# Attention values in a decoder layer: the high part of the probabilities times high and low values as one product of 128 columns

## What is computed

```python
x = x + attention(layernorm(x))
x = x + experts(layernorm(x))

# attention, for each sequence
q = ((h @ Wqa) @ Wqb)            # 16 heads of 64 + 64 (the second 64 rotated by position)
c_kv, k_pe = split(h @ Wkva)     # 64 latent values, 64 rotated keys per token
k, v = split(c_kv @ Wkvb)        # per head
scores = q @ k.T * scale         # causal
probs = softmax(scores)
out = (probs @ v) @ Wo
```

## Time and profile before

| | us |
|---|---|
| median of 3 runs | 1811.85 |
| lowest, highest | 1811.03, 1813.68 |
| profiled execution | 1815.64 |
| its span | 1813.8 |

### The profile page before, as it was taken

One profiled execution on the slowest core, in us unless ns is written; L12 is line 12 of the kernel. 1 busy time (PEld: TensorE's weight loads), 2 busy tenths in 40 slices (PEclk: granted clock), 3 DMA queues, 4 the chain that ended last, 5 costly groups with the idle time before them and its releaser, 6 DMA issues.

```text
span 1813.8 us, 45737 instructions
## 1 busy us (share of the span) xinstructions
PE 1549.9 (85%) x16420; PEld 1100.6 (61%) x16421; DVE 1311.4 (72%) x2969; ACT 1031.2 (57%) x2344; POOL 984.9 (54%) x1597
## 2 busy tenths in 40 slices
PE   7755788999878999998799999987999999889980
PEld 3233566766756667666567676665676666556650
DVE  1365886788768878887678788876877888555546
ACT  1343555666556666666566666664666666556650
POOL 3023566756457777554767756447776444343430
PEclk9777899999999999999999999998999999999995
DMA  6247441322234433123454321234432311356318
GB/s 167 76 110 109 80 72 38 56 57 57 53 74 83 94 63 60 23 51 59 76 102 74 63 55 39 36 64 92 86 60 57 57 30 25 99 148 210 114 32 280
DMA packets 333670, 144.19 MB, mean 79 GB/s; under 512 B 277168, under 2 KB 328403, under 8 KB 333398
## 3 DMA queue, kind: packets, MB, share of 16 engines
q1 hardware_dynamic: 308624, 105.54, 29.4%
q10 hardware_dynamic: 17926, 19.02, 3.6%
q0 software_dynamic: 6912, 16.83, 2.9%
HBM read 46.78 MB, written 29.53 MB: 42 GB/s over the span
## 4 chain that ended last, share of the span: by engine, by line
PE 51%; DVE 22%; ACT 6%; issue 6%; SPq 3%; DMA 3%; POOL 3%; DVEq 1%; ACTq 0%; POOLq 0%
PE of_ps L643 20%; PE s_ps L643 18%; PE t_ps L799 10%; DVE pT L1557 6%; DVE smax L1528 3%; ACT pT L989 2%; SPq L437 2%; DVE smax L1532 2%; DVE nmax L1536 1%; PE t_ps L882 1%; DVE nmax L1539 1%; ACT probs L1113 1%; DVE work L1363 1%; PE of_ps L899 1%; DVE smax L1510 1%
## 5 line engine op out<-in xcount | busy, mean ns | idle before, releaser
L1557 DVE TENSOR_TENSOR pT<-t_ps,pT 128x512 f16<-128x512 f32 (+3 forms) x688 | 409.7, 598 | 179.2 <-ACT pT L989 176.2
L989 ACT CAST pT<-t_ps 128x512 f16<-128x512 f32 (+3 forms) x688 | 355.1, 516 | 284.7 <-PE t_ps L799 283.4
L643 PE MATMUL s_ps<-kT,qT 128*128 128x512 f16 (+3 forms) x2304 | 492.5, 328 | 8.1 <-DMA kT<-ks_sb 4.1
L799 PE MATMUL t_ps<-id,probs 128*128 128x128 f32 x2304 | 384.5, 282 | 67.7 <-DVE pT L1557 28.2
L799 PEld LDWEIGHTS t_ps<-id,probs 128*128 128x128 f32 x2304 | 259.1, 143 | 167.5 <-issue 78.5
L1113 ACT ACTIVATE probs<-s_ps,nmax,fac 128x640 f32<-128x640 f32 (+3 forms) x256 | 269.2, 1052 | 2.2 <-DVE nmax L1536 2.2
L643 PE MATMUL of_ps<-weights,xT 128*128 128x512 f16 (+1 forms) x960 | 217.9, 366 | 59.8 <-DVE ks_sb L1352 23.0
L643 PEld LDWEIGHTS of_ps<-ckv,pT 128*128 128x128 f16 x6912 | 241.9, 98 | 42.8 <-DVE o_sb L1391 10.3
L643 PE MATMUL of_ps<-ckv,pT 128*128 128x64 f16 x6912 | 258.8, 193 | 7.9 <-DVE o_sb L1391 7.6
L643 PEld LDWEIGHTS s_ps<-kT,qT 128*128 128x128 f16 x2304 | 218.2, 99 | 76.8 <-issue 5.7
L643 PEld LDWEIGHTS of_ps<-weights,xT 128*128 128x128 f16 x960 | 83.3, 102 | 147.7 <-DVE ks_sb L1352 26.2
(11 more groups left out here) (218 smaller groups left out, 2504.6 us busy)
## 6 DMA issues: line engine op xcount, KB each, us to landing
wgu_sb<-wgu ACTq DMA_DIRECT2D x2, 2816.0 KB, 10.4
work<-lists SPq DMA_DIRECT2D x40, 128.5 KB, 2.1
qT<-lists SPq DMA_DIRECT2D x40, 128.5 KB, 2.1
x_sb<-x SPq DMA_DIRECT2D x32, 128.0 KB, 2.5
x<-x SPq DMA_DIRECT2D x32, 128.0 KB, 2.6
dense<-den SPq DMA_DIRECT2D x32, 128.0 KB, 2.7
weights<-dense ACTq DMA_DIRECT2D x1, 4096.0 KB, 21.5
qT<-y_exp SPq DMA_DIRECT2D x16, 256.0 KB, 5.1
```

Of the source, the lines that this page charges most:

```text
L643: return pe_.matmul(o, a, b, start=start, stop=stop)
L799: last = pe_.transpose(t_ps[:, h, c * P:(c + 1) * P], probs[:, u % 2, g * L + j * P:g * L + (j + 1) * P], id32[:, :])
L989: return act.copy(o, i)
L1557: dve.tensor_tensor(pT[:, u % 2, 1, h, 0:w], t_ps[:, h, 0:w], pT[:, u % 2, 0, h, 0:w], ALU.subtract).then_inc(s.lo_p, 1)
```

## The change

For i = 0 nothing changes in what is computed. For the others, the high part of the probabilities is multiplied with the high and low latent values side by side, one product of 128 columns in place of two of 64; the low part times the high values is added to the first 64 columns, as before. A head now takes 128 columns of `o_ps`, so the bank holds four heads, a quarter of a tile. The output therefore leaves in quarters (`out_quarter`): a reciprocal of 4 sums, a reduction that adds the two columns that lie 64 apart (512 values of PSUM to 256 in `o_sb`), and a multiply of the 256 values in `o_sb`. TensorE waits for a new semaphore, `o_taken`, which the reduction signals; `o_ready` is signalled by the multiply of the second and of the fourth quarter. The first and the third quarter wait for `lo_o`. They get places of their own, "quarter0" and "quarter2"; the second stands where the first half's `out_norm` was, the fourth where the second half's was.

```diff
+def parts(i):
+    return 2 if i == 0 else 4
+def part_of(t, k):
+    return sum(parts(j % TB) for j in range(t)) + k
 LONG = {... "half": (8, 3), "half_hi": (9, 0), "down": (10, 2),
+        "quarter0": (4, 3), "quarter2": (12, 3)}
 MIDDLE = {... "half": (4, 3), "half_hi": (5, 0), "out": (5, 2), "down": (7, 2),
+          "quarter0": (2, 3), "quarter2": (6, 3)}
 SECOND = {... "half": (3, 0), "half_hi": (3, 1), ... "down": (4, 0),
+          "quarter0": (2, 0), "quarter2": (4, 0)}
@@ values
-                if u % (U // 2) == 0 and 2 * t + u // (U // 2) > 0:
-                    pe_.wait_ge(s.o_ready, 2 * t + u // (U // 2))
+                step = U // parts(i)
+                if u % step == 0 and t + u > 0:
+                    pe_.wait_ge(s.o_taken, part_of(t, u // step))
...
-                        for a, b in ((0, 0), (0, 1), (1, 0)):
-                            last = mm(o_ps[:, head * C:(head + 1) * C], pT[:, u % 2, a, h, c * P:(c + 1) * P], ckv[:, b, j, :],
-                                      j == 0 and a + b == 0, j == i and a == 1)
+                        hi, lo = (pT[:, u % 2, a, h, c * P:(c + 1) * P] for a in range(2))
+                        if i == 0:
...
+                        else:
+                            head = o_ps[:, ((u * G + g) % (H // 4)) * 2 * C:][:, 0:2 * C]
+                            mm(head.rearrange("p (b c) -> p b c", b=2), hi, ckv[:, :, j, :], j == 0, False)
+                            last = mm(head[:, 0:C], lo, ckv[:, 0, j, :], False, j == i)
@@ before the experts
-            pe_.wait_ge(s.o_ready, 2 * NT)
+            pe_.wait_ge(s.o_taken, part_of(NT, 0))
@@ vector: behind the multiply of out_norm
+                dve.wait_ge(s.o_ready, half + 1)
+                dve.sem_inc(s.o_taken, 1)
+            def out_quarter(p, k):
+                U, half, at_ = units(p), 2 * p + k // 2, part_of(p, k)
+                dve.wait_ge(s.pv_made, unit_of(p, (k + 1) * (U // 4) - 1) + 1)
+                dve.reciprocal(rsum[:, 0:H // 4], ssum[:, p % 2, k * (H // 4):(k + 1) * (H // 4)]).then_inc(s.o_evs, 1)
+                if k % 2 == 0:
+                    dve.wait_ge(s.lo_o, half)
+                o4 = o_ps.rearrange("p (h b c) -> p h c b", b=2, c=C)
+                to = o_sb[:, (k % 2) * (H // 4) * C:][:, 0:(H // 4) * C].rearrange("p (h c) -> p h c", c=C)
+                dve.tensor_reduce(to, o4, AX_X, ALU.add).then_inc(s.o_taken, 1)
+                dve.wait_ge(s.o_taken, at_ + 1)
+                dve.wait_ge(s.o_evs, at_ + 1)
+                last = dve.tensor_tensor(to, to, rsum[:, 0:H // 4].unsqueeze(2).broadcast_to([P, H // 4, C]), ALU.mult)
+                if k % 2:
+                    last.then_inc(s.o_ready, 1)
+            def out_second(p, hh):
+                if p % TB == 0:
+                    out_norm(p, hh)
+                else:
+                    out_quarter(p, 2 * hh + 1)
@@ vector, side
                 if has(p) and (k, sub) == (0, 3):
-                    out_norm(p, 1)
+                    out_second(p, 1)
+                if t % TB and due("quarter0", t, t, k, sub):
+                    out_quarter(t, 0)
...
                 if due("half", t, t, k, sub):
-                    out_norm(t, 0)
+                    out_second(t, 0)
+                if t % TB and due("quarter2", t, t, k, sub):
+                    out_quarter(t, 2)
```

More of the change, by code:

```diff
@@ L86 @@
 LONG = {"lat": (0, 2), "pe0": (0, 3), "pe1": (1, 2), "q0": (2, 2), "q1": (3, 2), "gate": (5, 2), "up": (6, 2), "out": (7, 2),
-        "half": (8, 3), "half_hi": (9, 0), "down": (10, 2)}
+        "half": (8, 3), "half_hi": (9, 0), "down": (10, 2),
+        "quarter0": (4, 3), "quarter2": (12, 3)}
 MIDDLE = {"lat": (0, 1), "pe0": (0, 2), "pe1": (0, 3), "q0": (1, 2), "q1": (2, 2), "gate": (3, 2), "up": (4, 2), "half": (4, 3),
-          "half_hi": (5, 0), "out": (5, 2), "down": (7, 2)}
+          "half_hi": (5, 0), "out": (5, 2), "down": (7, 2),
+          "quarter0": (2, 3), "quarter2": (6, 3)}
 SECOND = {"lat": (0, 3), "pe0": (1, 1), "half_lo": (1, 1), "pe1": (1, 3), "out": (2, 0), "gate": (2, 1), "q0": (2, 2), "up": (2, 3), "q1": (3, 1),
-          "rope_sum": (3, 0), "half": (3, 0), "half_hi": (3, 1), "rope_hi": (3, 2), "rope_lo": (3, 3), "down": (4, 0)}
+          "rope_sum": (3, 0), "half": (3, 0), "half_hi": (3, 1), "rope_hi": (3, 2), "rope_lo": (3, 3), "down": (4, 0),
+          "quarter0": (2, 0), "quarter2": (4, 0)}
 FIRST_TILE = {"gate": (0, 0), "up": (0, 1), "pe0": (0, 2), "pe1": (0, 3), "lat": (1, 0), "q0": (1, 1), "q1": (1, 2), "out": (1, 3),
@@ L250, in build @@
                    s_made maxs max_ready exp_done p_made hi_p lo_p pv_made sum_done
-                   o_evs o_ready hi_o lo_o oT_in ln2_done x2T_in gate_done hi_h lo_h hT_in
+                   o_evs o_taken o_ready hi_o lo_o oT_in ln2_done x2T_in gate_done hi_h lo_h hT_in
                    lg_done top_s ix_ready pick_s mask_ready slot_s slot_done dense_done
@@ L814, in values @@
                     for c, (g, j) in enumerate(half_tiles(i, h)):
-                        head = (u * G + g) % (H // 2)
-                        for a, b in ((0, 0), (0, 1), (1, 0)):
-                            last = mm(o_ps[:, head * C:(head + 1) * C], pT[:, u % 2, a, h, c * P:(c + 1) * P], ckv[:, b, j, :],
-                                      j == 0 and a + b == 0, j == i and a == 1)
+                        hi, lo = (pT[:, u % 2, a, h, c * P:(c + 1) * P] for a in range(2))
+                        if i == 0:
+                            head = o_ps[:, ((u * G + g) % (H // 2)) * C:][:, 0:C]
+                            mm(head, hi, ckv[:, 0, j, :], True, False)
+                            mm(head, hi, ckv[:, 1, j, :], False, False)
+                            last = mm(head, lo, ckv[:, 0, j, :], False, True)
+                        else:
+                            head = o_ps[:, ((u * G + g) % (H // 4)) * 2 * C:][:, 0:2 * C]
+                            mm(head.rearrange("p (b c) -> p b c", b=2), hi, ckv[:, :, j, :], j == 0, False)
+                            last = mm(head[:, 0:C], lo, ckv[:, 0, j, :], False, j == i)
                 last.then_inc(s.pv_made, 1)
@@ L1386, in out_norm @@
                 dve.reciprocal(rsum[:, :], ssum[:, p % 2, hh * (H // 2):(hh + 1) * (H // 2)]).then_inc(s.o_evs, 1)
-                dve.wait_ge(s.o_evs, half + 1)
+                dve.wait_ge(s.o_evs, part_of(p, hh) + 1)
                 if half > 0:
@@ L1694, in hT_copy @@
                 dve.tensor_copy(m_hT_sb[:, :, :, :].rearrange("p a k n -> p (a k n)"), ot[0:KE, 0:4 * P]).then_inc(s.m_hTs, 1)
-            out_norm(NT - 1, 1)
+            out_second(NT - 1, 1)
             gate_hidden(NT - 2)
```

## The result

| | before | after |
|---|---|---|
| median us | 1812.8 (4 runs, 1811.0 to 1816.8) | 1860.3 (4 runs, 1858.4 to 1864.5) |
| profiled execution, its span | 1815.6, 1813.8 | 1858.7, 1856.9 |

The kernel after is slower: ratio 1.026, with an interval of 1.024 to 1.028. That is +48 us by the medians (47.6) and +43 by the profiled executions. The forecast was +37, its range 1812 to 1900.

The account below looks back on a forecast made before the run. TensorE was taken to bound the kernel, with VectorE close behind in longer tiles. New places 23, old places 16, GpSimd's low part 3, less 5 saved on TensorE, gave +37 us: 1849 from the median, range 1812 to 1900.

Parts of the forecast that it names:

- The saving on TensorE: One value product in place of two, 2240 pairs at 2.6 ns each: 5.8 us saved, taken as 5.
- The strided reduction: Rival: the quarters' reduction reads PSUM values 64 apart at half speed, a quarter takes 2.15 us: 1893; chance 0.16.
- New and old places at rest: Stalls with the multiply unstretched by GpSimd: 16 us at first and third quarters (new), 11 at second and fourth (old).
- The prediction's lower sum: Whole kernel with the multiply at rest and no wait for GpSimd: 16 + 11 - 5.8 = +21 us.
- the walk: At 56 new places, each low part's lateness minus its distance to the following transposes: 23 us, 16 at rest.
- GpSimd's low part: First and third quarters wait for it: 2.7 us in tile 4, first batch, 1 more at its third; 3 taken.
- The stretched multiply: Quarter's multiply of 256 values in SBUF, lengthened beside GpSimd: 0.61 us taken, 0.2 above rest; range 0.41 to 1.0.
- Who waits: Signs: idle time of TensorE's transposes behind L1557 grows some 20 us, ScalarE's wait for the output 13 to 16.
- By tile: Sign: the fifth to seventh tiles of a batch each grow by 1.5 to 2 us, the eighth least.

Follow-up runs that it names:

- the run with the multiply out of GpSimd's way: Kernel after with each quarter's multiply replaced by a one-input reduction of the same 256 values, output left undivided: 1837.0 us, ratio 1.013.
- the run with the late output: Kernel before with VectorE's signal to ScalarE for each half's output given 0.41 us later, TensorE released as before: 1826.8 us, ratio 1.006.
- the inserted steps alone: Kernel before with unused VectorE reductions put in at the 56 new places: 1819.9 us with one each (1.004), 1828.6 with two (1.008).
- both together: Kernel before with two unused reductions at each of 56 new places and the later signal to ScalarE at the old ones: 1868.2 us, ratio 1.020.
- the later session: Kernel after run again word for word, beside one with three narrow products: 1866.7 us, ratio 1.020 to the kernel before.

## Why the prediction was right, and where its sizes were off

**The saving on TensorE** (5 taken): the pace was right, 12 products in 0.67 us. The units' medians give 2 to 3 us that arrive; the runs' own medians differ too much among themselves to confirm it. The remark that TensorE isn't busy all the time was worth half of the term or more, not a sixth.

**The strided reduction**: 658 ns against 680 forecast, so that rival is out. The Trainium skill's rule on PSUM ("Advanced Engine Details and Errata", section Memory Cachelines) would have made it dearer; the trace differs for this read of 512 values by VectorE.

**New and old places at rest**: 16 and 11 forecast, 15 and 8 to 13 measured, each by a run of its own. With 2 to 3 saved by TensorE this gives +20 to 26, and the run with the multiply out of GpSimd's way gave +23. The prediction's lower sum, +21, was this case, so the walk held in its sum. Place by place it did less well (tile 3 at (2, 3) above), and part of the agreement is errors that cancel.

**GpSimd's low part** (3): one wait in the trace, 2.7 us, at tile 4 of the first batch, as forecast; the further 1 us for its third quarter isn't there.

**The stretched multiply** is the mis-sized term. The prediction added 0.2 us to each of the 112 multiplies, 22 us of VectorE's time, and had 12 of them paid (7 at the new places, 5 at the old). The trace has 0.17 us in the mean, 112 x (597 - 425) = 19 us: the amount was right. But 23 us were paid, nearly twice the term. The holds come in 37 pieces of up to 1.36 us, and what a piece costs goes by what GpSimd runs there and what stands behind it, not by the walk. The 1.36 us at (4, 3) of tile 5, where the walk had 0.14 to pay, cost 1.25 in every batch. Holds of 0.65 us at (2, 3) of tile 2 cost 0.5. Holds of 0.5 us at (2, 3) of tile 3 cost 1.8 to 1.97, since they push `nmax` into a hold of its own. Holds of 0.6 us behind the half outputs of tiles 2 and 3 cost nothing that TensorE's units show. So of the +9.3, +7.0 and +12.2 us at the places 2, 3 and 5, the multiply has 2.7, 8.2 and 7.4 (the first row of the table minus the second, lowered clocks included). At (12, 3) itself, the walk's main place, the forecast of 0.95 for tiles 4 to 6 was high: 0.56, 0.91 and 0.44 us in tiles 12 to 14, where the multiply took 0.57, 0.68 and 0.42 us.

**Who waits**: the transposes behind the low part have 23.5 us more, 20 forecast. ScalarE's wait for the output, L1430 and L1412 together (before, one line served all tiles), is 57.6 us in place of 47.2: 10 more, where 13 to 16 was forecast. A part doesn't show there, as ScalarE itself comes later where VectorE is late.

**By tile**: 1.5 to 2 us each was forecast for the fifth to seventh tiles and least for the eighth; it was 1.6, 3.0, 1.0 and 1.3 in the mean, so the sixth has most and the seventh least. The sixth has GpSimd's step of 2.13 us at its first quarter.

**What wasn't foreseen** is the clock, below, and that a hold can move another step under GpSimd. Of the 11 us by which the forecast was short (48 against 37), the multiply accounts for 11 (23 against 12), TensorE's saving for 2 to 3 more, and the new and old places, 15 and 8 to 13 against 16 and 11, for between 4 back and 1 more. The clock has no term of its own here: its share is inside these numbers.

## What to carry to other kernels

An instruction of VectorE with two SBUF inputs should be priced with what GpSimd's step at that place still has to go, not with a mean over the kernel: list the places, and look up GpSimd's step at each. Then look at the steps behind it, since a delay can bring another of them under GpSimd. In a list worked in order, a side job that waits costs by where it stands: the same cast three steps later was worth 1%, more than fusing 2240 pairs of products. Where an engine's units end in waits for other engines, fewer instructions on it bring a fraction of their own time, even where it has 44% of the chain.

## What the runs showed of the hardware

**A short wait behind which the clock falls.** In tile 13 of the kernel after, TensorE idled 1.85 us behind the first half's output (1.42 at the same place before). Then its granted clock was at half, the lower of the two levels (1.2 GHz in place of 2.4). The timeline, and the two stretches by busy time, granted clock and DMA:

```profile
726.11 1.04 PE L812 MATMUL t_ps<-id,probs 128*128 128x128 f32 x4 [1.85 <-ACT probs L1134]
...
726.95 1.49 PE L656 MATMUL s_ps<-kT,qT 128*128 128x512 f16 x3
```

```profile
722.00:726.00 4.00, 2.26 (x25) 1.50 (x22) 2.76 (x8) 2.03 (x5) 3.16 (x11) 1.00 0.00 0
726.00:730.00 4.00, 3.89 (x20) 2.75 (x21) 2.25 (x5) 2.26 (x6) 3.48 (x6) 0.57 0.17 33
730.00:734.00 4.00, 4.00 (x49) 3.44 (x47) 3.45 (x13) 1.83 (x4) 3.23 (x7) 1.00 0.33 66
```

The three score products take 1.49 us in place of 0.81. The stretch lasts 3.4 us and costs about 1.6 (2.05 lost by tile 15's unit in the run with the late output, 0.45 of it the delay). In tiles 4 to 7, in one traced execution each, the kernel before has none, the kernel after six, the late output alone three, the inserted steps alone none, both together seven. The kernel after has ten in the later session, so the count varies. Four of its six stand behind the half output, one at the first quarter of tile 4, where VectorE waits 2.7 us for GpSimd, and one late in tile 31. So most of them come with the delay behind the half output, and the steps at the new places alone bring none. The length of the idle time by itself doesn't decide: tile 12 of the kernel after idled 1.87 us at the same point and kept its full clock, tiles 5 and 29 idled the 1.85 us of tile 13 and kept it too, and tile 15 lost it behind 1.35 and 0.36. What else decides is open. For the +48 us the six are some 10, an estimate. They aren't beside the 23 of the multiply and the 13 of the late output but inside them; the run without the multiply has five.

**Reading values 64 apart from PSUM** costs VectorE nothing in a reduction: 658 ns for 512 values, 682 in a row.

**A product whose moving operand is two runs of 64 values** goes at the pace of whole 128 columns, about 56 ns: 12 products, half of them of 64 columns, take 0.67 us, and 0.19 for the last one's length plus 6 x 56 and 5 x 29.3 ns makes 0.67.

**A step of VectorE held by GpSimd** ends about 0.28 us after GpSimd's step in 34 of 37 multiplies of 256 values, whether that step took 0.2 or 2.5 us.
